# Attention and feed-forward kernel: fp16 split made in token order and turned by DMAs, denominators summed partly on TensorE

## The chip, the cores and the metric

The kernel runs on one core of one Trainium2 chip. The metric is the device time of one execution in microseconds (us). Engines are named as in the profile: PE is TensorE (PEld its weight loads), DVE is VectorE, ACT is ScalarE, POOL is GpSimd and SP is SyncE, whose queue (SPq) issues nearly all DMAs.

## What is computed

x is 8 x 512 x 1024 and the context is 8 x 512 x 256, in fp32. Cut to what matters, the reference is

```
q  = layernorm(x)                                # rows of 1024: 8 key heads x 4 query groups x 32
s  = q_head @ ctx_head.T / sqrt(32)              # 512 x 512 for each batch, key head and group
x1 = x + softmax(s) @ ctx_head
z  = layernorm(x1)                               # then 8 experts: one gate each, best one taken
out = x1 + (1 - g) * z + g * (bias[e] + degen[e] @ (update[e].T @ (z - debias[e])))
```

## The kernel before

**Units.** The attention is cut into 64 units (8 batches x 8 key heads). A unit has 16 score tiles of 128 keys x 512 queries, n = 0 to 15: four key blocks t for each of the 4 query groups. The unit loop is walked in four steps t = 0 to 3. For each score tile, TensorE makes it from 97 rows (`score_keys`, L589: fp16 high and low parts of both operands stacked, and one row with the shift that keeps the exponent small), ScalarE exponentiates it into `probs` (L884), and TensorE multiplies the probabilities with the values (`gather`, L603). The shift is the negative row maximum of approximate scores: TensorE makes them from the high parts alone (L551, four banks of PSUM), VectorE reduces them (`row_max`, L949), TensorE turns the 16 maxima (L634), ScalarE scales them (L795), and SP sends them by a small DMA into the last row of `q_stack` (`send_shift`, L406). This runs ahead: step t = 2 of unit u begins the maxima of unit u+2, and the shift of unit u+1 is sent within unit u.

**Denominators.** GpSimd adds the probability tiles of key blocks 0 and 1 (L363) and those of 2 and 3 (L351), 2048 columns each; TensorE sums both results over the keys with a matrix of ones (L616, L626), VectorE turns the total into `den_t` (L961) and inverts it (L967), and GpSimd scales the output rows and adds x (L323, L328).

**PSUM.** Four banks hold the approximate scores, one the output, and three banks serve by turns the score tiles, the turned maxima, the denominators and, before the change, the turned parts of x. A plan in the code (`filled`, `KEPT`, `bank_of`) gives each use its bank; TensorE waits (`bank_free`) until the use before it in that bank has been read.

**The split.** For each of the 32 token tiles of 128 rows: VectorE takes the moments, ScalarE centres x (L802) and scales it (L809), TensorE turns x and the context in ten 128 x 128 blocks (L577), ScalarE writes the high fp16 part times 16 (L820, L824) and VectorE the low part (L1002, L1008). Pairs of tiles are stored to DRAM (`q_split`, `k_split`) and loaded again by unit (`load_unit`, L68 to L76: 8 DMAs). Five tiles are made before the loop; the other 27 one per two units, the last in unit 51.

**SP's queue** runs a hand-written order: waits, then issues, one behind the other. The last stage (the feed-forward part) follows unit 63.

## Time and profile before

| what | value |
|---|---|
| median of 3 runs | 1024.77 us (1020.37 to 1025.66) |
| the profiled execution, first to last instruction (its span) | 1023.9 us |
| PE busy | 949.4 us (93%) |
| DVE busy | 904.8 us (88%) |
| ACT busy | 761.3 us (74%) |
| POOL busy | 794.4 us (78%) |
| SP queue | 161.76 MB, 64.3% of 16 DMA engines |

The profile gives no other time of the profiled execution than its span; the span lies 0.9 us under the median. Busy time of PE counts matmuls that overlap, so 93% is not 93% of its peak.

### The profile page before, as it was taken

The page shows a single profiled execution, that of the slowest core. Times are in us where ns is not written, and L with a number is a line of the kernel's source. Part 1 is how long each engine was busy: PE and PEld are TensorE (multiplying, and loading weights), DVE is VectorE, ACT ScalarE, POOL GpSimd, SP SyncE. Part 2 cuts the span into 40 slices and gives each one's busy share as a digit, 9 for nine tenths or more (in the row PEclk, how much of TensorE's full clock was granted, in tenths as well). Part 3 has the DMA queues.
Part 4 walks back from the last instruction along what each step waited for, and adds up shares of the span by engine and source line. Part 5 has one row for each costly group of instructions (what it writes and reads, how often), then busy time and mean ns, then how long its engine had stood idle before and what let it go on. Part 6 is the DMA issues. An engine that isn't in the chain of part 4 may idle for free.

```text
span 1023.9 us, 24706 instructions
## 1 busy us (share of the span) xinstructions
PE 949.4 (93%) x9518; PEld 372.5 (36%) x9518; DVE 904.8 (88%) x1138; ACT 761.3 (74%) x1333; POOL 794.4 (78%) x422
## 2 busy tenths in 40 slices
PE   4789999999999999999999999999999999999996
PEld 3223233333333232333333333332222226777773
DVE  6869999999999999999999999998888876888976
ACT  7468888888888888888888888888777777554440
POOL 7158999999999999999999999998999998222110
PEclk9989999999999999999999999999999999999998
DMA  7675677767677767676767686766555744766423
GB/s 247 184 167 114 161 154 168 156 162 159 155 158 167 168 152 170 145 171 150 180 143 175 138 188 134 182 122 154 119 119 139 165 95 141 247 213 236 148 104 164
DMA packets 319876, 164.19 MB, mean 160 GB/s; under 512 B 182216, under 2 KB 307240, under 8 KB 319760
## 3 DMA queue, kind: packets, MB, share of 16 engines
q1 hardware_dynamic: 319456, 161.76, 64.3%
q8 instruction: 76, 1.25, 0.5%
q0 software_dynamic: 304, 0.85, 0.3%
q14 instruction: 40, 0.33, 0.1%
HBM read 107.58 MB, written 54.53 MB: 158 GB/s over the span
## 4 chain that ended last, share of the span: by engine, by line
PE 36%; DVE 30%; issue 25%; ACT 5%; POOL 2%; DMA 1%; SPq 0%; DVEq 0%; POOLq 0%; ACTq 0%
DVE row_max L949 14%; PE psum L589 8%; PE psum L603 6%; PE psum L616 5%; PE psum L734 5%; DVE den_t L961 4%; PE psum L551 4%; ACT probs L884 3%; PE psum L712 3%; DVE o_t L955 3%; PE psum L577 2%; DVE probs L1161 2%; DVE prod_mem L1008 2%; PE psum L700 1%; ACT prod_mem L824 1%
## 5 line engine op out<-in xcount | busy, mean ns | idle before, releaser
L884 ACT ACTIVATE probs<-psum 128x512 f32<-128x512 f32 x1024 | 554.7, 596 | 106.7 <-PE psum L589 88.7
L949 DVE TENSOR_REDUCE row_max<-psum 128x4 f32<-128x2048 f32 x248 | 566.0, 2282 | 63.5 <-PE psum L551 63.1
L589 PE MATMUL psum<-q_stack,k_stack 97*32 97x512 f16 x4096 | 335.0, 386 | 10.2 <-issue 3.6
L363 POOL TENSOR_TENSOR sums<-probs 128x2048 f32<-128x2048 f32 x63 | 287.8, 4568 | 19.5 <-ACT probs L884 19.5
L351 POOL TENSOR_TENSOR sums<-probs 128x2048 f32<-128x2048 f32 x63 | 287.2, 4558 | 10.2 <-PE psum L626 5.5
L603 PE MATMUL psum<-probs,v_in 128*32 128x512 f32 x2048 | 268.9, 598 | 1.0
L589 PEld LDWEIGHTS psum<-q_stack,k_stack 97*32 97x32 f16 x4096 | 96.8, 95 | 258.7 <-ACT probs L884 148.6
L551 PE MATMUL psum<-high_mem 32*128 32x512 f16 x992 | 98.3, 385 | 23.7 <-DVE row_max L949 20.0
L323 POOL TENSOR_TENSOR o_t<-o_t,inv 128x512 f32<-128x512 f32 x64 | 67.1, 1048 | 44.2 <-DVE inv L967 44.2
L328 POOL TENSOR_TENSOR o_all<-o_all,o_t 128x512 f32<-128x512 f32 x64 | 81.5, 1274 | 9.5 <-POOL o_t L323 0.4
L603 PEld LDWEIGHTS psum<-probs,v_in 128*32 128x32 f32 x2048 | 59.4, 111 | 61.1 <-issue 16.7
L551 PEld LDWEIGHTS psum<-high_mem 32*128 32x128 f16 x992 | 26.8, 91 | 138.3 <-DVE row_max L949 83.2
L335 POOL TENSOR_SCALAR var_eps<-mv 128x1 f32<-128x1 f32 x32 | 9.3, 290 | 82.2 <-DVE mv L1036 81.6
L626 PE MATMUL psum<-sums,ones 128*32 128x512 f32 x512 | 68.1, 604 | 0.0
L734 PE MATMUL psum<-down,probs 128*128 128x512 f32 x128 | 64.3, 632 | 3.9 <-DVE probs L1161 3.1
L616 PE MATMUL psum<-sums,ones 128*32 128x512 f32 x512 | 67.5, 597 | 0.0
L712 PE MATMUL psum<-w_all,high_mem 128*128 128x136 f32 x512 | 64.8, 280 | 1.1 <-ACT high_mem L897 1.1
L712 PEld LDWEIGHTS psum<-w_all,high_mem 128*128 128x128 f32 x512 | 62.2, 191 | 5.2 <-issue 4.1
L577 PE MATMUL psum<-ident,xa 128*128 128x128 f32 x256 | 45.3, 310 | 16.0 <-ACT xa L809 10.5
L824 ACT ACTIVATE prod_mem<-psum 128x512 f16<-128x512 f32 x60 | 35.8, 597 | 32.0 <-PE psum L577 32.0
L897 ACT ACTIVATE high_mem<-psum 128x1024 f32<-128x1024 f32 x32 | 32.4, 1013 | 29.5 <-PE psum L700 29.5
L955 DVE STREAM_TRANSPOSE o_t<-psum 128x512 f32<-128x512 f32 x64 | 44.3, 692 | 8.2 <-PE psum L603 4.3
(120 smaller groups left out, 788.9 us busy)
## 6 DMA issues: line engine op xcount, KB each, us to landing
q_stack<-q_split SPq DMA_DIRECT2D x192, 128.0 KB, 3.4
xa<-in_x_dram SPq DMA_DIRECT2D x32, 512.0 KB, 4.7
o_all<-in_x_dram SPq DMA_DIRECT2D x256, 64.0 KB, 2.5
x_attended<-o_all SPq DMA_DIRECT2D x64, 256.0 KB, 4.1
out_dram<-probs SPq DMA_DIRECT2D x32, 512.0 KB, 2.9
q_split<-prod_mem SPq DMA_DIRECT2D x15, 1024.0 KB, 5.4
xa<-x_attended SPq DMA_DIRECT2D x16, 512.0 KB, 4.5
probs<-x_attended SPq DMA_DIRECT2D x16, 512.0 KB, 5.3
```

The costliest lines, as they stand in the source:

```text
L328: pool.tensor_tensor(o_all[:, half, :, h, :], o_all[:, half, :, h, :], turned_rows, ALU.add).then_inc(o_made, 1)
L351: pool.tensor_tensor(sums[:, (2 * u - 1) % SUMS], probs[:, (u - 1) % 2, 2], probs[:, (u - 1) % 2, 3], ALU.add).then_inc(back_done, 1)
L363: pool.tensor_tensor(sums[:, 2 * u % SUMS], probs[:, u % 2, 0], probs[:, u % 2, 1], ALU.add).then_inc(front_done, 1)
L551: last = pe.matmul(s_ps[:, g, :], q_high[rows, u % SLOTS, t * P:(t + 1) * P], k_high[rows, u % SLOTS, :], start=True, stop=True)
L589: last = pe.matmul(st_ps[row:row + D, bank_of["score", u, n], :], k_stack[:, u % SLOTS, t * P + row:t * P + row + D], q_stack[:, u % SLOTS ...
L603: last = pe.matmul(o_ps[g * D:(g + 1) * D, :], v_in[:, u % 2, t, :], probs[:, u % 2, t, g, :], start=(t == 0), stop=(t == ST - 1))
L616: pe.matmul(st_ps[g * D:(g + 1) * D, bank_of["den", u, 0], :], ones[:, 0:D], sums[:, 2 * u % SUMS, g, :], start=True, stop=False)
L712: last = pe.matmul(z_ps[:, t % 2, 0:WC], yT[:, t % 2, c, :], w_all[:, c, :], start=(c == 0), stop=(c == EC - 1))
L734: last = pe.matmul(result_bank(n)[:, half * 512:(half + 1) * 512], mixT[:, t, :], down[:, half * 512:(half + 1) * 512], start=True, stop=True)
L884: act.activation(probs[:, s, keys, g, :], st_ps[:, bank_of["score", u, n], :], ACT.Exp, scale=EXP_SCALE).then_inc(exped, 1)
L949: dve.reduce_max(row_max[:, u % 2, t:G * ST:ST], s_ps[:], AX.X).then_inc(reduced, 1)
L955: dve.transpose(o_t[:, u % 2, :], o_ps[:]).then_inc(o_taken, 1)
```

## The change

The split is made in token order: ScalarE writes the high part of the context (L846), normalises x in place in one pass that also multiplies by 16 (L851) and copies it to fp16 (L859). The low parts are subtractions: on VectorE for the first five tiles, on GpSimd (L284, L287, L291) for the others. Four DMAs per tile, issued by SP (`turn_x`, L410, and `turn_c`, L421), turn the fp16 parts; TensorE's ten transposes and the reads of PSUM behind them are gone. GpSimd adds only key blocks 0 and 1; TensorE sums blocks 2 and 3 straight from `probs`, so a unit has three groups of denominator matmuls (`denominators`, L667) in steps 0 and 1 of the following unit. The positions of the fp16 work among ScalarE's tiles, the bank plan, SP's order and the number of x tiles loaded ahead (6) are new; the folding of constants moves from before unit 0 into units 1 to 3.

```diff
+            C_SPLIT_AT, CENTRE_AT, HIGH_AT, SHIFT_AT = 4, 6, 2, 8
...
-                    filled += scores[half:]
...
                         filled.append(("den", u - 1, 0))
-            KEPT = {"score": 2, "max": 2, "den": (5, 5), "part": 6}
+                    if live(u):
+                        filled += [("score", u, n) for n in range(G * t, G * (t + 1))]
+            KEPT = {"score": 2, "max": 2, "den": 9}
             bank_of, bank_before, free_at, last_in = {}, {}, [0] * BANKS, [None] * BANKS
             for i, use in enumerate(filled):
...
+                def low_parts(n):
+
+                    pool.wait_ge(c_high, n + 1)
+                    pool.tensor_scalar(c_tile(n), c_tile(n), UP, None, ALU.mult).then_inc(c_scaled, 1)
+                    turned(pool, split_before(n), "c")
+                    pool.wait_ge(c_scaled, 2 * (n - FIRST) + 1)
+                    pool.tensor_tensor(c_parts(n)[:, 1], c_tile(n), c_parts(n)[:, 0], ALU.subtract
+                                       ).then_inc(c_scaled, 1)
+                    turned(pool, split_before(n), "x")
+                    pool.wait_ge(x_high, n + 1)
+                    pool.tensor_tensor(x_parts(n)[:, 1], x_tile(n), x_parts(n)[:, 0], ALU.subtract
+                                       ).then_inc(low_done, 1)
 
...
+                for u in range(-AHEAD, UNITS + 1):
+                    if u % 2 == 0 and whole(tile_of(u)) and u > -AHEAD:
+                        inverse_root(tile_of(u))
+                    if u % 2 == 1 and whole(tile_of(u)):
+                        low_parts(tile_of(u))
...
-                    if live(u - 2):
-                        normalise(u - 2)
...
-                        pool.tensor_tensor(sums[:, 2 * u % SUMS], probs[:, u % 2, 0], probs[:, u % 2, 1],
+                        pool.tensor_tensor(sums[:, u % SUMS], probs[:, u % 2, 0], probs[:, u % 2, 1],
                                            ALU.add).then_inc(front_done, 1)
...
+                    if live(u - 1):
+                        normalise(u - 1)
...
+                def turn_x(n, part):
+
+                    if part == 0:
+                        sp.wait_ge(x_high, n + 1)
+                        if n % 2 == 0 and n >= ST:
+                            sp.wait_ge(split_out, stored(n // 2))
+                    else:
+                        low_made(sp, n)
+                    landed = turned_first["x"][n] if n < FIRST else turned_in["x"][n % 2]
+                    cols = slice(n % 2 * P, (n % 2 + 1) * P)
+                    sp.dma_start_transpose(q_parts_of(n)[:, part, :, cols], x_parts(n)[:, part]).then_inc(landed, 16)
+
+                def turn_c(n):
+
+                    if n < FIRST:
+                        sp.wait_ge(c_low, n + 1)
+                    else:
+                        sp.wait_ge(c_scaled, 2 * (n - FIRST + 1))
+                    landed = turned_first["c"][n] if n < FIRST else turned_in["c"][n % 2]
+                    cols = slice(n % 2 * P, (n % 2 + 1) * P)
+                    for part in range(2):
+                        sp.dma_start_transpose(k_parts_of(n)[:, part, :, cols], c_parts(n)[:, part]
+                                               ).then_inc(landed, 16)
+
                 def load_first_highs(pair):
 
                     last = 2 * pair + 1
...
                 sp.wait_ge(early_out, 32)
                 load_unit(sp, 1, "highs")
                 load_unit(sp, 0)
                 load_v(0)
-                load_x(FIRST + 2)
+                turn_c(ST)
+                turn_x(ST, 0)
+                turn_x(ST, 1)
                 send_shift(0)
...
                 load_unit(sp, 2)
                 load_unit(sp, 3)
-
-                for u in range(-AHEAD, UNITS + 2):
+                sp.wait_ge(zeroed, 3)
+                sp.dma_start(down[NE:NE + NX, :], bias_w).then_inc(b_in, 16)
+                sp.dma_start(c_part[0:1, WC:WC + NX], imp_center.rearrange("(o n) -> o n", o=1)).then_inc(b_in, 16)
+                sp.dma_start(c_part[0:1, WC + NX:], imp_slope.rearrange("(o n) -> o n", o=1)).then_inc(b_in, 16)
+                for n in range(UPFRONT + 1, UPFRONT + FIRST):
+                    load_x(n)
...
+                        for g in ((2, 3), (), (0,), (1,))[u % HALF]:
+                            load_addend((u + 2) // HALF, g)
+                    if u % 2 == 0 and n + UPFRONT - 1 < TILES and u > -AHEAD:
+                        load_x(n + UPFRONT - 1)
+                    if u % 2 == 1 and whole(n):
+                        turn_x(n, 0)
+                        turn_x(n, 1)
+                        turn_c(n)
+                    if live(u) and live(u + 1):
                         send_shift(u + 1)
...
+                def denominators(u, i):
+
+                    if i == 0:
+                        bank_free("den", u, 0)
+                    terms = (probs[:, u % 2, 2], sums[:, u % SUMS], probs[:, u % 2, 3])[i]
+                    if i == 1:
+                        pe.wait_ge(front_done, u + 1)
                     else:
-                        pe.wait_ge(front_done, u + 1)
-                    bank_free("den", u, 0)
-                    wait(pe, den_taken, u)
-                    for g in range(G):
-                        pe.matmul(st_ps[g * D:(g + 1) * D, bank_of["den", u, 0], :], ones[:, 0:D],
-                                  sums[:, 2 * u % SUMS, g, :], start=True, stop=False)
-
-                def last_denominators(u):
-
...
-                        if u == -1 and t == 2:
-                            turn_max(0)
+                        if t == 2 and live(u + 1):
+                            turn_max(u + 1)
...
+                        if t == 0 and live(u - 1) and live(u):
+                            denominators(u - 1, 0)
+                        if t == 1 and live(u - 1) and live(u):
+                            denominators(u - 1, 1)
+                        if t == ST - 1 and live(u):
+                            gather(u, 1)
...
+                            score_keys(u, G * t, G * t + 2)
+                        if t == 0 and live(u - 1):
+                            gather(u - 1, ST - 1)
+                        if t == 1 and live(u - 1) and live(u):
+                            denominators(u - 1, 2)
+                        if t == 2 and live(u):
+                            gather(u, 0)
+                        if t == ST - 1 and live(u):
+                            gather(u, 2)
+                        if live(u):
+                            score_keys(u, G * t + 2, G * (t + 1))
 
...
+                def split_context(n):
+
+                    x_landed(act, n)
+                    if n >= ST:
+                        turned(act, split_before(n), "c")
+                    act.activation(c_parts(n)[:, 0], c_tile(n), ACT.Copy, scale=UP).then_inc(c_high, 1)
+
+                def normalise_tile(n):
+
+                    act.wait_ge(rstd_done, 2 * n + 2)
+                    act.activation(x_tile(n), x_tile(n), ACT.Identity, scale=rstd[:, n % 2:n % 2 + 1],
+                                   bias=neg_mean[:, n % 2:n % 2 + 1]).then_inc(xn_done, 1)
+
+                def high_part(n):
+
+                    act.wait_ge(xn_done, n + 1)
+                    if n >= ST:
+                        turned(act, split_before(n), "x")
+                    act.activation(x_parts(n)[:, 0], x_tile(n), ACT.Copy).then_inc(x_high, 1)
+
+                for n in range(FIRST):
+                    split_context(n)
+                    normalise_tile(n)
+                    high_part(n)
 
...
+                        if even and n == C_SPLIT_AT:
+                            split_context(tile)
+                        if even and n == CENTRE_AT:
+                            normalise_tile(tile)
+                        if odd and n == HIGH_AT:
+                            high_part(tile)
...
+                        if n == SHIFT_AT and live(u + 1):
                             make_shift(u + 1)
...
-                        if t == 0 and live(u - 2) and u % 2 == 0:
-                            take_denominators(u - 2)
...
-                        if t == 1 and live(u - 2):
-                            invert(u - 2)
...
+                        if t == 1 and live(u - 1) and live(u):
                             take_denominators(u - 1)
+                            invert(u - 1)
```

On TensorE, in the steps t = 0 and 1 of an even unit before the change (the rows begin in step 3 of the unit before; L616 and L626 are the denominators of that unit):

```order
L551 MATMUL psum<-high_mem 128x512 x4
L589 MATMUL psum<-q_stack,k_stack 32x512 x8
L603 MATMUL psum<-probs,v_in 32x512 x4
L634 MATMUL psum<-ident,row_max 16x128
L589 MATMUL psum<-q_stack,k_stack 32x512 x8
L616 MATMUL psum<-sums,ones 32x512 x4
L551 MATMUL psum<-high_mem 128x512 x4
L626 MATMUL psum<-sums,ones 32x512 x4
L589 MATMUL psum<-q_stack,k_stack 32x512 x8
```

Two groups of four denominator matmuls stood there, and the score tiles behind the second (L589) waited for probabilities to be read, not for the denominators. After the change the second and third group stand in step 1 of the unit (L637 is now `score_keys`; rows shown with what they wait for):

```order
L667 MATMUL psum<-sums,ones 32x512 [waits front_done]
L667 MATMUL psum<-sums,ones 32x512 x3
L637 MATMUL psum<-q_stack,k_stack 32x512 [waits exped]
L637 MATMUL psum<-q_stack,k_stack 32x512 x3
L637 MATMUL psum<-q_stack,k_stack 32x512 [waits exped]
L637 MATMUL psum<-q_stack,k_stack 32x512 x3
L667 MATMUL psum<-probs,ones 32x512 [waits exped]
L667 MATMUL psum<-probs,ones 32x512 x3
L637 MATMUL psum<-q_stack,k_stack 32x512 [waits den_taken]
L637 MATMUL psum<-q_stack,k_stack 32x512 x3
```

The third group sums `probs` directly; the second score tile pair of step 1 (tiles 6 and 7) comes straight behind it, and the plan gives tile 6 the bank of the denominators, so it waits until VectorE has read them (`den_taken`).

On SP, the last issues before the shift of unit 1 is sent (`send_shift(1)`, the last row; the same three-way load of a unit, 8 DMAs, stands ahead for unit 2, and 6 more for unit 1) were before the change:

```order
L68 DMA high_mem<-q_split 128x512
L69 DMA high_mem<-k_split 128x1x512
L74 DMA q_stack<-q_split 32x4x512 x3
L76 DMA k_stack<-k_split 32x512 x3
L431 DMA o_all<-in_x_dram 32x16x32 x4
L398 DMA q_split<-prod_mem 128x16x256
L400 DMA k_split<-k_parts 128x4x256
L412 DMA v_in<-in_ctx_dram 128x4x32
L406 DMA q_stack<-shift 1x16x128
```

After the change the loads of units 1, 2 and 3 stand as before behind `send_shift(0)`; between them and the rows below come three small constants and the loads of x tiles 7 to 10 (8 DMAs); then

```order
L477 DMA o_all<-in_x_dram 32x16x32 x8
L410 DMA_TRANSPOSE prod_mem<-xa 128x8x128 x2
L421 DMA_TRANSPOSE k_parts<-c_split 128x2x128 x2
L444 DMA q_split<-prod_mem 128x16x256
L446 DMA k_split<-k_parts 128x4x256
L458 DMA v_in<-in_ctx_dram 128x4x32
L477 DMA o_all<-in_x_dram 32x16x32 x8
L397 DMA xa<-in_x_dram 128x1024
L398 DMA cin<-in_ctx_dram 128x256
L452 DMA q_stack<-shift 1x16x128
```

Between `send_shift(0)` and `send_shift(1)` stood 29 DMAs, and now 58: the new ones are three constants, ten of x and context loads, 12 addends (`o_all`) and four transposing ones. Ahead of `send_shift(0)` stood 40 and stand 55.

## Rows read from the trace of the kernel before

**Rows 1.** Windows: busy us of PE, PEld, DVE, ACT, POOL, clock, DMA share.

```profile
400.00:500.00 100.00, 96.32 (x1064) 30.49 (x1064) 93.42 (x88) 84.11 (x155) 92.57 (x36) 1.00 0.71 159
...
700.00:800.00 100.00, 92.81 (x1072) 27.96 (x1072) 86.99 (x62) 74.62 (x143) 93.38 (x33) 1.00 0.62 138
```

**Rows 2.** Timeline of GpSimd, second addition of units two apart (start us, us).

```profile
408.36 4.56 POOL L351 TENSOR_TENSOR sums<-probs 128x2048 f32<-128x2048 f32 x1
...
433.68 4.56 POOL L351 TENSOR_TENSOR sums<-probs 128x2048 f32<-128x2048 f32 x1
...
760.40 4.57 POOL L351 TENSOR_TENSOR sums<-probs 128x2048 f32<-128x2048 f32 x1 [0.40 <-PE psum L626]
...
784.52 4.57 POOL L351 TENSOR_TENSOR sums<-probs 128x2048 f32<-128x2048 f32 x1 [0.40 <-PE psum L626]
```

**Rows 3.** Timeline of TensorE in units without split work.

```profile
757.85 1.05 PE L616 MATMUL psum<-sums,ones 128*32 128x512 f32 x8
758.83 0.39 PE L551 MATMUL psum<-high_mem 32*128 32x512 f16 x4
759.15 1.07 PE L626 MATMUL psum<-sums,ones 128*32 128x512 f32 x8
760.03 0.62 PE L589 MATMUL psum<-q_stack,k_stack 97*32 97x512 f16 x8
760.47 1.04 PE L603 MATMUL psum<-probs,v_in 128*32 128x512 f32 x8
761.33 0.77 PE L589 MATMUL psum<-q_stack,k_stack 97*32 97x512 f16 x8
...
774.16 0.40 PE L551 MATMUL psum<-high_mem 32*128 32x512 f16 x4 [0.52 <-DVE row_max L949]
...
777.04 0.40 PE L551 MATMUL psum<-high_mem 32*128 32x512 f16 x4 [0.65 <-DVE row_max L949]
...
778.78 0.28 PE L634 MATMUL psum<-ident,row_max 128*16 128x128 f32 x1
```

**Rows 4.** Timeline of VectorE in the same units.

```profile
771.18 0.70 DVE L961 STREAM_TRANSPOSE den_t<-psum 128x512 f32<-128x512 f32 x1
...
774.64 2.25 DVE L949 TENSOR_REDUCE row_max<-psum 128x4 f32<-128x2048 f32 x1
```

**Rows 5.** Timeline of ScalarE in the same units.

```profile
775.01 2.30 ACT L884 ACTIVATE probs<-psum 128x512 f32<-128x512 f32 x4 [0.46 <-PE psum L589]
```

**Rows 6.** Waits over the whole run (us in total, times, longest).

```profile
PEld psum L589 <- DVE den_t L961: 7.8, 36, 0.2
```

**Rows 7.** Groups by line over the whole run (busy us, mean ns, idle before).

```profile
L363 POOL TENSOR_TENSOR sums<-probs 128x2048 f32<-128x2048 f32 x63 | 287.8, 4568 | 19.5 <-ACT probs L884 19.5
...
L577 PE MATMUL psum<-ident,xa 128*128 128x128 f32 x256 | 45.3, 310 | 16.0 <-ACT xa L809 10.5 <-DVE prod_mem L1008 5.0
...
L1008 DVE SCALAR_TENSOR_TENSOR prod_mem<-psum,prod_mem 128x512 f16<-128x512 f32 x60 | 40.7, 679 | 3.1 <-ACT prod_mem L824 3.1
L802 ACT ACTIVATE xa<-xa,neg_mean 128x1024 f32<-128x1024 f32 x32 | 36.8, 1150 | 0.8 <-DVE var_eps L994 0.8
```

**Rows 8.** Timeline of SP's queue between the shifts of units 0 and 1.

```profile
41.22 0.57 SPq L406 DMA_DIRECT2D q_stack<-shift  x1
41.83 1.53 SPq L74 DMA_DIRECT2D q_stack<-q_split  x3
...
61.13 0.89 SPq L406 DMA_DIRECT2D q_stack<-shift  x1
```

**Rows 9.** Timeline of TensorE: first score tiles of units 0 and 1.

```profile
46.38 1.04 PE L589 MATMUL psum<-q_stack,k_stack 97*32 97x512 f16 x8
...
63.56 1.05 PE L589 MATMUL psum<-q_stack,k_stack 97*32 97x512 f16 x8 [3.64 <-issue]
```

**Rows 10.** Timeline of SP's queue in the middle of the loop.

```profile
406.57 2.14 SPq L400 DMA_DIRECT2D k_split<-k_parts  x1
...
416.03 2.17 SPq L431 DMA_DIRECT2D o_all<-in_x_dram  x4
...
421.09 0.38 SPq L68 DMA_DIRECT2D high_mem<-q_split  x1
...
425.06 0.42 SPq L412 DMA_DIRECT2D v_in<-in_ctx_dram  x1
```

373 lines of the change are left out of this document (142 added, 231 removed).

## The prediction

> **What bounds the kernel now.** I read the windows first, for the stages. Mid-loop PE is busy 96 of 100 us, VectorE 93, GpSimd 93 and ScalarE 84; in the units without split work 93, 87, 93 and 75 [rows 1]. No engine is alone the bound, so shares don't tell what a change is worth. The period does: GpSimd's second addition of the same unit parity comes at 408.36 and 433.68, 25.32 us for two units with one tile to split, and at 760.40 and 784.52, 24.12 us for two without [rows 2]. All the work of splitting thus costs 1.20 us per pair, whatever its busy time.
>
> Next the timelines of one unit, to see what a step is made of. TensorE's own lengths, start to start [rows 3]: the approximate scores 0.32 (758.83 to 759.15), a group of denominators 0.88 (0.98 ahead of approximate scores), two score tiles 0.44, a group of values 0.86. VectorE's reduction takes 2.25 and ends at 776.89; the next approximate scores start at 777.04, 0.15 us later [rows 3, 4]. From 774.16 to 777.04 that loop takes 2.88 us: the floor of a step, since the four banks of the approximate scores serve TensorE and VectorE by turns. Before, both limits lie close: steps of 2.9 to 3.4 us, by TensorE's content or this loop. ScalarE's tiles follow each other at (2.30 - 0.60)/3 = 0.57 us [rows 5], 9.1 us a unit, with room.
>
> What reading the denominators costs now: TensorE's score tiles waited for it 7.8 us in all, 0.2 us at most [rows 6]. They are read well before a score tile needs their bank.
>
> Last SP. Between the shifts of units 0 and 1 it sends 30 DMAs in 19.91 us (41.22 to 61.13), 0.66 us each, almost without a pause; the shift is needed, and unit 1's first scores start at 63.56, 2.43 us after its issue began [rows 8, 9]. At the start SP's queue sets the time.
>
> **The change part by part, a steady unit.** Removed from TensorE: 10 transposes a tile; added: one group of denominators a unit, 0.88 us. By content its four steps are now, in the order of the new code: step 0, scores 0.32, denominators 0.88, two tiles, values, two tiles, 2.94 us; step 1, 0.32 + 0.88 + 0.44 + 0.88 + 0.44 = 2.96; step 2 is short, and the loop with VectorE holds it at 2.88; step 3, 0.32 + 0.86 + 0.44 + 0.86 + 0.44 = 2.92.
>
> Two waits come on top. First, while the denominators hold one of three banks, score tiles have two. In step 0 the tiles start at 1.20; ScalarE takes the second from 2.21 to 2.81, TensorE wants its bank at 2.72: 0.14 us, step 0 is 3.08. Second, and larger: tile 6 stands right behind the third group and takes over the denominators' bank. In step 1 that group starts at 1.64 and ends 1.07 later, at 2.71 (length in [rows 3]); VectorE's reduction, begun 0.48 after the scores (774.16, 774.64), ends at 2.73, so it isn't late; it reads from 2.77 for 0.70 us [rows 4], TensorE resumes 0.15 us later, at 3.62 instead of 2.52. The 1.10 us is full loss, as no engine has work stored: the next approximate scores stand behind this wait. With two tiles and the turned maxima (issue taken as 0.21 from their 0.28 [rows 3]) the next step starts at 4.27. Before, this wait was 0.2 us at most. The unit: 3.08 + 4.27 + 2.88 + 2.92 = 13.15 us.
>
> Split work. ScalarE: one pass of 1.15 us less [rows 7]; of what is left, the context part and the normalising pass of even units lie in front of tiles 4 and 6, in ScalarE's idle time during the wait just described: nothing. The fp16 copy of odd units lies ahead of tile 2: tiles 2 and 3 come about 1.1 us later, so tiles 4 and 5 find their banks late and the third group starts about 0.45 us late, which moves the whole wait: +0.45 a pair. VectorE loses 0.68 us x 2 and a context part, work that hid in the reductions' gaps: no gain beside the 2.88 floor. GpSimd loses 4.57 us a unit and gets a low part; by its 512-column rate (half the 2048-column addition's 4.57 would be 1024 columns, 2.3 us [rows 7]) plus two context steps some 3.5 us a pair: about 18 of 26 us, and its remaining addition ends some 3 us before TensorE asks. Nothing, unless GpSimd has other waits. TensorE's transposes, 45.3 us in all [rows 7], are in the step sums already.
>
> So a pair takes 26.30 us, 26.75 with a tile, against 24.12 and 25.32. Units 1 to 51 are 25 pairs with a tile: 25 x 1.43 = 36; units 52 to 62, 5.5 pairs x 2.18 = 12. Sum +48 us.
>
> **The turning DMAs.** The trace has none. Below, one costs SP what a small DMA does, 0.42 us; above, what a held-up one does, 2.14 us [rows 10]. I take 0.66, the mean of SP's busy stretch, as these have 64 to 256 KB. In an odd unit SP loads a unit (421.09 to 425.06, 3.97 us), values 0.42, four addends 2.17 [rows 10]: 6.6 us; the low parts are ready at about 6.4; four turning DMAs 2.6, the shift 2.43 to be used: 11.7. It is needed at 13.15 + 1.20 = 14.35. Hidden, with 2.7 us of cover; at 2.14 each it arrives at 17.6 and costs 3.3 us a pair.
>
> Advanced Engine Details and Errata (the Trainium skill, section X-Bar Transpose) says that transposing DMAs are about as fast as plain ones. By that rule the 0.66 stands and the sum doesn't move; no row here shows it.
>
> **The start.** Ahead of the first shift stand 15 DMAs more, 0 to 15 x 0.66 = 10 us (SP also waited here, so some fit in); the turned parts now pass through DMAs before anything is stored or scored, so I take +8: first shift at 49.2. From there 58 DMAs instead of 29 stand ahead of the second: 59 x 0.66 = 39.2, shift 1 at 88.4, unit 1 at 90.8 against 63.56: +27 us. TensorE, ScalarE and VectorE all stop there: the score tiles that wait for the shift stand ahead of everything else on TensorE. Bounds: 59 x 0.42 with no delay ahead gives +5; 1.0 us each (the transfers of 10 loads held up) +50. Folding constants inside units 1 to 3 adds three waits of TensorE for a copy, some 1 us each: +3. The last stage is the same: 0.
>
> DMA: Bandwidth & Descriptors (the Trainium skill, section Issuing engines are not separate DMA queues) says that issue time is usually small against the transfer. That would leave out this term: rival 2 below has its time. Against it, here SP issues nearly without pause and the reader waits.
>
> **Sum.** 27 + 3 + 48 = 78. The profiled span is 1023.9, the median 0.9 above it: 1024.8 + 78 = 1103 us.
>
> **Rivals.** (1) Turning DMAs dear to issue, 2.14 us each: the shift is late in 25 odd units, 25 x 3.3 = 82, and 4 x 1.5 at the start: 1191 us. For it: SP has little room. Against: SP reads no data. It decides from about 1.3 us each. Chance 0.18. (2) Only one of the two new waits is real. Without the start term: 1076. Without the bank wait a pair is 24.1, 24.55 with a tile: 25 x -0.77 = -19, and with the start 1024.8 + 30 - 19 = 1036. For it: banks may come free otherwise than I count. Chance 0.20. (3) Faster: VectorE's read is early enough (the point is 1.1 us earlier in step 1), and SP's extra issues lie in its waits: 1024.8 - 19 + 3 = 1009, down to 985 if steps lose their other waits too. Against it: the order of code puts the read right ahead of tile 6, whatever the speeds. Chance 0.12. (4) Gains and losses cancel within 0.5%, about what a measurement of this kernel can tell from no change: 0.04. My forecast: 0.46, its own range 1075 to 1130.
>
> The range that leaves out 2 in 10: from 1022 (rival 3 and part of 4 below it) to 1180 (half of rival 1 above). Faster 0.12, same 0.04, slower 0.84.
>
> **What would show it.** The first score tiles of unit 1 at 85 to 95 us, with SP issuing from 50 on; GpSimd's additions 26 to 27 us apart per pair mid-loop and about 26.3 late; TensorE's score line waiting for `den_t` 62 times, some 1 us each, 60 to 70 us in all; shift DMAs issued before 12 us of an odd unit; GpSimd busy near 50%. The prediction is wrong if that wait is missing, if the period is under 25.3, or if a turning DMA occupies SP over 1.3 us.

## The result and the profile after

The changed kernel takes 1214.48 us (median of 4 runs, 1210.49 to 1218.13) against 1023.07 for the kernel before (median of 4, 1020.37 to 1025.66): 1.187 times, 95% interval 1.183 to 1.192. It is slower, as forecast, but by 191 us and not by 78, and above the range. The profiled execution took 1216.57 us, its span is 1214.8 us.

Read the period first, as in [rows 2]. GpSimd's one addition a unit is the mark (timeline of GpSimd, kernel after: start us, busy us, and in brackets the idle time before it):

```profile
564.91 4.56 POOL L378 TENSOR_TENSOR sums<-probs 128x2048 f32<-128x2048 f32 x1 [9.30 <-ACT probs L911]
578.48 4.55 POOL L378 TENSOR_TENSOR sums<-probs 128x2048 f32<-128x2048 f32 x1 [2.46 <-ACT probs L911]
591.96 4.56 POOL L378 TENSOR_TENSOR sums<-probs 128x2048 f32<-128x2048 f32 x1 [5.61 <-ACT probs L911]
611.81 4.55 POOL L378 TENSOR_TENSOR sums<-probs 128x2048 f32<-128x2048 f32 x1 [4.56 <-ACT probs L911]
626.50 4.55 POOL L378 TENSOR_TENSOR sums<-probs 128x2048 f32<-128x2048 f32 x1 [6.83 <-ACT probs L911]
...
1016.65 4.55 POOL L378 TENSOR_TENSOR sums<-probs 128x2048 f32<-128x2048 f32 x1 [6.41 <-ACT probs L911]
1030.05 4.57 POOL L378 TENSOR_TENSOR sums<-probs 128x2048 f32<-128x2048 f32 x1 [6.42 <-ACT probs L911]
```

Two kinds of units stand here. Late in the loop a unit takes 13.40 us. In the middle units of 13.57 and 13.48 us are followed by one of 19.85 and one of 14.69: 61.6 us for four, where before had 2 x 25.32 = 50.6 [rows 2]. The steady unit of the prediction (13.15 us) exists; a second thing comes on top of it once in four units. The windows say the same of the means, against [rows 1] (busy us of PE, PEld, DVE, ACT, POOL, granted clock, DMA share, GB/s): every engine is less busy, TensorE 82 of 100 us, and the bound is none of them.

```profile
400.00:500.00 100.00, 82.04 (x870) 23.29 (x862) 72.73 (x58) 63.29 (x119) 54.74 (x35) 0.95 0.78 160
700.00:800.00 100.00, 83.15 (x899) 23.85 (x903) 76.42 (x59) 64.41 (x121) 62.04 (x38) 0.97 0.73 148
```

**The clean unit.** TensorE, kernel after, from a score tile of step 0 to the start of step 2, to be set beside [rows 3]:

```profile
571.17 0.62 PE L637 MATMUL psum<-q_stack,k_stack 97*32 97x512 f16 x8
...
573.17 0.39 PE L614 MATMUL psum<-high_mem 32*128 32x512 f16 x4
573.49 1.07 PE L667 MATMUL psum<-sums,ones 128*32 128x512 f32 x8
574.37 0.78 PE L637 MATMUL psum<-q_stack,k_stack 97*32 97x512 f16 x8
574.98 1.03 PE L667 MATMUL psum<-probs,ones 128*32 128x512 f32 x8
576.86 0.61 PE L637 MATMUL psum<-q_stack,k_stack 97*32 97x512 f16 x8 [0.85 <-DVE den_t L984]
577.41 0.28 PE L686 MATMUL psum<-ident,row_max 128*16 128x128 f32 x1
577.62 0.39 PE L614 MATMUL psum<-high_mem 32*128 32x512 f16 x4
```

Step 1 runs from 573.17 to 577.62, 4.45 us where 4.27 were forecast. The third group of denominators ends at 576.01, and score tile 6 stands behind it until VectorE has read `den_t`. The list of waits (us in all, times, longest) has it 63 times. It lists matmuls (PE) and their weight loads (PEld) apart; the two overlap and aren't to be added up. [Rows 6] had 7.8 us for the weight loads:

```profile
PEld psum L637 <- issue: 221.8, 376, 24.2
...
PEld psum L637 <- DVE den_t L984: 110.3, 63, 1.8
...
PE psum L637 <- issue: 82.6, 25, 23.1
...
PE psum L637 <- DVE den_t L984: 53.1, 63, 0.8
```

The two rows with "issue" hold the second thing: score matmuls that wait for something for which the trace names no releasing engine. The matmuls do so 25 times, 82.6 us in all, the longest 23.1 us at the start. It is the shift, a row of the score stack that SP must send (experiment 2 moves nothing else).

**The long unit.** SP's queue and TensorE, kernel after (SP: start, us of issuing, DMAs). The shift of a unit is L452:

```profile
576.80 3.03 SPq L410 DMA_TRANSPOSE prod_mem<-xa  x2
579.87 3.11 SPq L421 DMA_TRANSPOSE k_parts<-c_split  x2
583.03 0.58 SPq L452 DMA_DIRECT2D q_stack<-shift  x1
...
592.47 5.05 SPq L477 DMA_DIRECT2D o_all<-in_x_dram  x8
...
598.57 0.59 SPq L452 DMA_DIRECT2D q_stack<-shift  x1
...
602.21 1.05 PE L637 MATMUL psum<-q_stack,k_stack 97*32 97x512 f16 x8 [3.80 <-issue]
603.01 1.95 PE L653 MATMUL psum<-probs,v_in 128*32 128x512 f32 x8
...
605.75 0.61 PE L614 MATMUL psum<-high_mem 32*128 32x512 f16 x4
```

Between two shifts SP issues almost without a pause for 15.5 us, longer than a clean unit: the stores of the turned pair, the eight loads of a unit, the values, eight addend loads, a tile and its context. The score tile starts 3.64 us behind the shift's issue, after a wait of 3.80 us. Issue isn't all of it: this shift took 3.5 us to land, those at 583.03 and 617.56 took 1.7. The DMA engines were busy 0.88 to 0.96 of the time behind this one, and 0.05 and 0.25 behind the other two (windows from 583 to 585 and from 617 to 620). No experiment takes this longer landing apart from the late issue. And the wait costs more than itself: what follows it runs slower. Windows of the kernel after:

```profile
598.00:602.00 4.00, 0.41 (x4) 0.00 (x0) 1.76 (x1) 0.00 (x0) 2.46 (x3) 0.87 0.88 231
602.00:604.00 2.00, 1.79 (x16) 0.72 (x20) 0.00 (x0) 1.05 (x3) 0.00 (x0) 0.50 0.96 213
```

The granted clock is 0.50 from 602 on, the 1.2 GHz level, and was back at 1.00 in the window from 608; TensorE had done hardly anything since 598.4. A group of values then takes 1.95 us, and 1.04 in the same place of other units. From the first late tile to the next step it is 3.54 us (602.21 to 605.75) where the clean unit takes 2.00; with what step 1 loses some 2.3 us.

**The turning DMAs.** The rows that the kernel before could not show, 60 of the 64 DMAs of each line (ns of issue on SP: least, median, most; the other eight have medians of 1322 and 1244):

```profile
L410 SPq DMA_TRANSPOSE prod_mem<-xa x60: 1231/1331/4798, 11.6 to 878.9; - x60
L421 SPq DMA_TRANSPOSE k_parts<-c_split x60: 1222/1248/2302, 9.0 to 881.6; - x60
```

1.33 us for one of 256 KB and 1.25 us for one of 64 KB, about twice the assumed 0.66. They land 3.8 and 2.4 us (medians) from their issue.

**The start.** SP and TensorE, kernel after, against [rows 8, 9]:

```profile
52.37 0.36 PE L601 MATMUL psum<-high_mem 32*128 32x256 f16 x1 [52.37 <-DMA high_mem<-probs]
...
67.01 0.59 SPq L452 DMA_DIRECT2D q_stack<-shift  x1
...
84.83 8.05 SPq L477 DMA_DIRECT2D o_all<-in_x_dram  x8
103.03 5.08 SPq L477 DMA_DIRECT2D o_all<-in_x_dram  x8
...
109.16 0.59 SPq L452 DMA_DIRECT2D q_stack<-shift  x1
...
112.64 1.04 PE L637 MATMUL psum<-q_stack,k_stack 97*32 97x512 f16 x8 [23.11 <-issue]
```

The first shift goes out at 67.01 instead of 41.22, the second at 109.16, and unit 1's first score tile starts at 112.64 instead of 63.56: +49 us. The first shift is late since its maxima are: the first row is TensorE's first approximate scores, which began at 27.36 before and now wait until 52.37 for parts that passed through turning DMAs.

**The budget.** GpSimd's first additions of unit 0 and of unit 62 start at 53.7 and 840.0 before and at 76.2 and 1030.0 after. So the span's +190.9 us are +22.5 up to unit 0's mark, +26.8 between the marks of units 0 and 1 (18.3 before, 45.1 after), +140.7 in the 61 units after that (768.0 and 908.7), and +0.9 behind the last mark.

### The profile page after: what moved, and what is told of

Read it like the earlier page. It is cut to its first block, busy times and chain, and to the rows that moved or that the text cites. A ratio compares the mean times of both kernels' runs of the same rounds, so it can differ in the third digit from the quotient of the medians.

```text
span 1214.8 us, 24979 instructions
## 1 busy us (share of the span) xinstructions
PE 971.3 (80%) x9702; PEld 352.8 (29%) x9702; DVE 892.2 (73%) x1020; ACT 715.5 (59%) x1269; POOL 614.4 (51%) x472
## 4 chain that ended last, share of the span: by engine, by line
PE 64%; DVE 20%; issue 9%; SPq 4%; DMA 2%; ACT 1%; POOL 1%; DVEq 0%; POOLq 0%; ACTq 0%
PE psum L637 17%; PE psum L667 15%; PE psum L653 15%; DVE row_max L972 12%; PE psum L614 7%; PE psum L778 4%; DVE den_t L984 4%; PE psum L756 3%; DVE probs L1172 2%; PE psum L744 1%; PE psum L686 1%; SPq L410 1%; DMA cin<-in_ctx_dram 1%; SPq L421 1%; SPq L76 0%
## 5 line engine op out<-in xcount | busy, mean ns | idle before, releaser
L637 PE MATMUL psum<-q_stack,k_stack 97*32 97x512 f16 x4096 | 347.9, 395 | 141.9 <-issue 82.6
L378 POOL TENSOR_TENSOR sums<-probs 128x2048 f32<-128x2048 f32 x63 | 287.2, 4559 | 323.6 <-ACT probs L911 323.6
L653 PE MATMUL psum<-probs,v_in 128*32 128x512 f32 x2048 | 279.8, 619 | 2.3 <-ACT down L823 1.3
L637 PEld LDWEIGHTS psum<-q_stack,k_stack 97*32 97x32 f16 x4096 | 106.4, 97 | 518.6 <-issue 221.8
L667 PE MATMUL psum<-probs,ones 128*32 128x512 f32 x1008 | 132.8, 599 | 0.0
L291 POOL TENSOR_TENSOR xa<-xa 128x1024 f16<-128x1024 f32 x27 | 57.7, 2137 | 83.9 <-ACT xa L859 83.9
L653 PEld LDWEIGHTS psum<-probs,v_in 128*32 128x32 f32 x2048 | 61.9, 112 | 45.4 <-ACT probs L911 15.6
L667 PE MATMUL psum<-sums,ones 128*32 128x512 f32 x504 | 71.3, 640 | 0.0
L984 DVE STREAM_TRANSPOSE den_t<-psum 128x512 f32<-128x512 f32 x64 | 45.9, 717 | 9.9 <-PE psum L667 8.0
L601 PE MATMUL psum<-high_mem 32*128 32x256 f16 x2 | 0.8, 376 | 53.7 <-DMA high_mem<-probs 52.4
```

The lines of the kernel that those rows point to most:

```text
L378: pool.tensor_tensor(sums[:, u % SUMS], probs[:, u % 2, 0], probs[:, u % 2, 1], ALU.add).then_inc(front_done, 1)
L637: last = pe.matmul(st_ps[row:row + D, bank_of["score", u, n], :], k_stack[:, u % SLOTS, t * P + row:t * P + row + D], q_stack[:, u % SLOTS ...
L653: last = pe.matmul(o_ps[g * D:(g + 1) * D, :], v_in[:, u % 2, t, :], probs[:, u % 2, t, g, :], start=(t == 0), stop=(t == ST - 1))
L667: last = pe.matmul(st_ps[g * D:(g + 1) * D, bank_of["den", u, 0], :], ones[:, 0:D], terms[:, g, :], start=(i == 0), stop=(i == 2))
L984: dve.transpose(den_t[:], st_ps[:, bank_of["den", u, 0], :]).then_inc(den_taken, 1)
```

## The experiments

Fourteen kernels ran; each is the kernel after with one edit, or a sum of such edits. The kernel before took 1022.6 to 1024.7 us (medians) beside them. Times are medians of 2 to 5 runs, and gains are counted from the 1214.5 us of the kernel after where nothing else is said.

**1. Take away the wait for the bank.** The planner keeps the denominators' bank for 11 score parts, and the turned maxima move behind the score tiles of step 2, so that tile 6 gets another bank.

```
-            KEPT = {"score": 2, "max": 2, "den": 9}
+            KEPT = {"score": 2, "max": 2, "den": 11}
...
-                        if t == 2 and live(u + 1):
-                            turn_max(u + 1)
...
+                        if t == 2 and live(u + 1):
+                            turn_max(u + 1)
```

> The bank of the denominators is given on later (kept 11 uses, so the turned maxima take it over, not score tile 6), and the maxima are turned behind the approximate scores of step 2. If the wait of tile 6 is what lengthens the clean units (13.4 us in the late stage), tile 6 no longer waits for den_t (163 us in all in the changed kernel), a clean unit takes 12.2 to 12.4 us, and the late units 52 to 62 alone give back 11 to 13 us; in the middle SP's queue may hold the units up instead, so the whole is 15 to 65 us faster. Rival: the units are held by VectorE's loop or TensorE's content, and the wait only shows where they would stop anyway: late units stay at 13.4 us, total within 10 us.

Measured: 1203.4 us, ratio 1.176 (1.172 to 1.179). TensorE's wait for `den_t` is gone from the list, and a late unit is 1.09 us shorter (timeline of GpSimd):

```profile
978.33 4.57 POOL L378 TENSOR_TENSOR sums<-probs 128x2048 f32<-128x2048 f32 x1 [5.32 <-ACT probs L911]
990.64 4.57 POOL L378 TENSOR_TENSOR sums<-probs 128x2048 f32<-128x2048 f32 x1 [5.33 <-ACT probs L911]
```

12.31 us against 13.40. But the whole gained only 11 us, under the 15 to 65 expected: in the middle a unit of 12.13 us was followed by ones of 14.50 and 19.65, so the gain was waited away at the next shifts. The wait is real, and this kernel can't price it.

**2. The shift first.** SP sends the shift right behind the values' load, ahead of stores, addends, tile loads and turning DMAs.

```
                     if live(u) and live(u + 1):
                         load_v(u + 1)
+                        send_shift(u + 1)
...
-                    if live(u) and live(u + 1):
-                        send_shift(u + 1)
```

> SP sends each shift right behind the load of the values, ahead of the addends, the x loads and the turning DMAs. If the shift's place in SP's queue is what costs the middle units 6 to 7 us per four units, most of it goes, 40 to 90 us in all, and the start (unit 1 at 112.6 us) comes 5 to 8 us earlier, as the eight addends and one x load of unit 0 no longer stand ahead. Rival: SP is simply full (over 50 of 60 us issuing per four units), the order moves the delay onto the unit loads and the total changes by under 20 us or grows.

Measured: 1188.3 us, ratio 1.161 (1.149 to 1.173), 26 us gained, where 40 to 90 were expected. One long unit in four is left. What holds it now, SP and TensorE of this kernel:

```profile
563.30 0.41 SPq L444 DMA_DIRECT2D q_split<-prod_mem  x1
...
572.42 0.60 SPq L452 DMA_DIRECT2D q_stack<-shift  x1
...
575.86 0.62 PE L636 MATMUL psum<-q_stack,k_stack 97*32 97x512 f16 x8 [2.70 <-issue]
```

The store of the turned pair, L444, starts 1.2 us behind the last turning DMA, when these have landed, and it, its fellow and the unit's loads still stand ahead of the shift.

**3 and 7. Thin out the start.** In the third the constants, the tiles 7 to 11 and the first 16 addends go behind unit 1's shift; in the seventh the same with tile 7 left ahead.

```
-                for n in range(UPFRONT + 1, UPFRONT + FIRST):
-                    load_x(n)
...
+                    if u == 0:
...
+                        for m in range(UPFRONT + 1, UPFRONT + FIRST):
+                            load_x(m)
+                        for g in (0, 1, 2, 3):
+                            load_addend(0, g)
```

> The three constants, the x loads 7 to 11 and the 16 addends of unit 0 go behind the shift of unit 1. If SP's queue sets the start, unit 1's first score tile comes at 80 to 90 us instead of 112.6 and the total is 20 to 30 us less. Rival: the loads and addends are needed at once behind it and the delay is only moved to unit 2 or 3: total within 8 us of the changed kernel.

> As e3_start, but x tile 7 is still loaded ahead, since VectorE's moments of that tile stood in front of unit 0's maxima and kept them waiting until 97 us. If the queue ahead of the second shift is what costs the start, unit 1 begins at 92 to 96 us instead of 112.6 and the total falls by 12 to 20 us; unit 2 may wait again, since the moved DMAs stand ahead of its shift. Rival: the whole stall moves to unit 2 as before and the total stays within 5 us.

Measured: 1214.7 us, ratio 1.187 (1.183 to 1.190), and 1213.9, ratio 1.185 (1.182 to 1.189): nothing. The timeline of TensorE, the seventh, shows where the gain went:

```profile
94.43 1.05 PE L642 MATMUL psum<-q_stack,k_stack 97*32 97x512 f16 x8 [6.35 <-issue]
...
121.78 1.04 PE L642 MATMUL psum<-q_stack,k_stack 97*32 97x512 f16 x8 [11.36 <-issue]
```

Unit 1 starts 18 us earlier (94.43 for 112.64), and unit 2 waits for its own shift behind the work put off. Work moved behind one shift on a full queue stands ahead of the next.

**4. Plain copies in place of the turning DMAs**, same bytes, same places; the parts are then not transposed.

```
-                    sp.dma_start_transpose(q_parts_of(n)[:, part, :, cols], x_parts(n)[:, part]).then_inc(landed, 16)
+                    sp.dma_start(q_parts_of(n)[:, part, :, cols], x_parts(n)[:, part].rearrange("p (h s) -> p h s", s=P)).then_inc(landed, 16)
```

> The 128 turning DMAs are plain copies of the same bytes to the same places, so the parts are not transposed and the result is not the attention's; the work and its order are the same. If what hurts is SP's time to issue a turning DMA (1.25 to 1.33 us each), each takes 0.45 to 0.6 us now, SP has 100 us less to issue, and the total falls by 60 to 110 us. Rival: what hurts is the bytes moved inside SBUF or the waits around them: the issue time falls but the total by under 30 us.

Measured: 1166.7 us, ratio 1.140 (1.137 to 1.143), 48 us gained, under the 60 to 110 expected; issue times of this kernel:

```profile
L410 SPq DMA_DIRECT2D prod_mem<-xa x60: 594/684/2514, 11.5 to 833.3; - x60
```

0.68 us, what I had assumed for a turning one. By medians the 128 DMAs give back 64 x 0.65 + 64 x 0.45 = 70 us of issue, and two thirds of it show in the time. Twice the price is a large cause, not the whole one.

**5. One turning DMA for the high and the low part together**, 64 instead of 128.

```
-                    sp.dma_start_transpose(q_parts_of(n)[:, part, :, cols], x_parts(n)[:, part]).then_inc(landed, 16)
+                    sp.dma_start_transpose(q_parts_of(n)[:, :, :, cols].rearrange("p l h s -> p (l h) s"),
+                                           x_parts(n).rearrange("p l e -> p (l e)")).then_inc(landed, 16)
```

> One turning DMA per tile for both parts of x and one for both parts of the context, 64 instead of 128, the same bytes. If a turning DMA costs SP a fixed 1.25 to 1.33 us, as the equal times for 256 KB and 64 KB say, each still takes 1.3 to 1.5 us, SP has 80 us less to issue, and the total falls by 30 to 60 us, as with the plain copies (49 us). Rival: the issue time grows with the blocks turned (16 instead of 8 in one DMA), each x one takes 2.6 us and the total stays within 15 us.

Measured: 1180.4 us, ratio 1.153 (1.149 to 1.156), 34 us gained.

```profile
L408 SPq DMA_TRANSPOSE prod_mem<-xa x30: 1788/2032/5372, 12.3 to 844.1; - x30
```

2.03 us for 512 KB against 2 x 1.33: part of the price goes by the DMA, part by its size.

**6. The addends issued by GpSimd**, which is idle half the time: `load_addend` moves from SP's program into GpSimd's, ahead of the tile's inverse root and low parts.

```
+                    if live(u + 2):
+                        for g in ((2, 3), (), (0,), (1,))[u % HALF]:
+                            load_addend((u + 2) // HALF, g)
```

> The 256 addend loads are issued by GpSimd (half idle) instead of SP; the bytes and the engines that move them are the same. If SP's issue time is what is short, SP loses 2.2 to 2.9 us a unit and the total falls by 50 to 90 us, the start included (16 addends stood ahead of the second shift, 8 to 13 us). Rival 1: the DMA engines are the limit and nothing changes, within 15 us. Rival 2: GpSimd takes about 1 us for each, 4 us a unit, and delays its own sums: the clean units rise above 13.6 us.

Measured: 1222.1 us, ratio 1.193 (1.188 to 1.199): no gain, and 8 us lost if anything, as the interval touches that of the kernel after (1.183 to 1.192). Unit 1's mark comes 4.6 us earlier, and the 61 units behind it take 8 us longer. GpSimd's timeline:

```profile
587.56 5.19 POOL L373 DMA_DIRECT2D o_all<-in_x_dram  x8
```

0.65 us each. In the even unit the tile's inverse root and mean stand behind these eight. ScalarE's normalising pass waits 1.98 us for them and TensorE 1.89 us for ScalarE, and the unit takes 15.39 us. In odd units the low parts come later behind four addends: SP's turning DMAs wait for them 14 times, 25.0 us in all, where the kernel after had one such wait of 0.4. That an engine is idle half the time doesn't make it a free queue.

**8. The edits 1 and 2 together.**

> The bank change (15 us when alone) and the earlier shift (30 us when alone) together. If the bank change gained little because SP held the middle units up, more of it shows now: clean units at 12.3 us, total 55 to 85 us below the changed kernel. Rival: SP is full, its work per four units (about 53 us) is a floor, and shorter units only wait longer: 35 to 45 us below, the sum of both or less.

Measured: 1159.7 us, ratio 1.132 (1.117 to 1.148). 55 us gained, where the two had given 11 and 26 apart. Still one unit in four is long, 15.4 to 18.9 us.

**9. The stores of the turned pair behind the shift too**, on top of 8.

```
-                    if u % 2 == 0 and (n - 1) % 2 == 1 and FIRST <= n - 1 < TILES:
-                        store_split(n - 1)
...
                         send_shift(u + 1)
+                    if u % 2 == 0 and (n - 1) % 2 == 1 and FIRST <= n - 1 < TILES:
+                        store_split(n - 1)
```

> As e8_bank_shift (shift sent right behind the v load, den word kept 11 parts), but the stores of the pair of turned tiles are issued behind the shift. In e8 one unit of four lasted 18.6 us: the sync engine's queue held two pairs of turning DMAs (5.2 us), then stood 2.5 us until they had landed, issued the stores (2.2 us), the eight loads of unit u+3 (5.5 us) and the v load, and only then the shift (617.67), and TensorE's next score tile came 4.84 us late. My theory: that wait and the stores are what makes the one long unit; without them the shift goes out 4.6 us earlier, the long unit drops to about 14 us, four units take 53 to 54 us instead of 57.3, and the time falls by about 55 us to 1100 us (1090 to 1115). Rival: the sync engine's pure issue time per four units (about 53 us) is already the bound, so the delay only moves to another unit: time 1130 to 1155. Second rival: what is late is the landing of the unit loads, not their issue: no change, 1160.

Measured: 1145.3 us, ratio 1.119 (1.113 to 1.125), 14 us under 8, with intervals that overlap. My theory missed by 45 us, and the number is the first rival's: that SP's issue time itself is near the bound. In the trace SP issues for 13.2 us a unit (400 to 700 us). The next two test it.

**10. Merged turning DMAs on top of 9** (the edit of 5), and **11. plain copies on top of 9** (the edit of 4).

> As e9_store_late, and each tile's high and low part are turned by one DMA, 2 per tile instead of 4. In e5 the merged one took 2.03 us to issue for x against 2 x 1.33, and about 1.3 to 1.5 for the context against 2 x 1.25, so four units cost the sync engine 3 to 4 us less. If the sync engine's issue time is the bound: 25 to 45 us faster than e9, about 1065 (1050 to 1085). If it no longer bounds in e9, only the start gains: 10 to 15 us, 1085.

> As e9_store_late, with the turning DMAs replaced by plain copies of the same bytes, so that the parts are not transposed and the output is not the reference's. 0.6 to 0.7 us each to issue instead of 1.25 to 1.33. This is about the floor of this order of work with all turning at the plain price: loop units 12.3 to 12.7 us, 1030 to 1060 us. If it stays above e10, something else than the issue time (landing, the clock) holds the loop.

Measured: 1096.1 us, ratio 1.071 (1.067 to 1.075), and 1093.6, ratio 1.070 (1.067 to 1.073). 49 and 52 us gained over 9, more than the 25 to 45 expected; the times themselves missed, 1096 against 1050 to 1085 and 1094 against the floor of 1030 to 1060. Both relieve SP by about 2 us a tile and both end at the same time, so SP's issue ahead of the shifts holds this loop. But single units stay long in 11 too (14 to 15.6 us), so the price of turning isn't all of it.

**12. The first 16 addends and the constants issued by GpSimd in unit 0**, on top of 10.

```
+                    if u == 0:
+                        for g in range(4):
+                            first_addend(0, g)
+                        pool.wait_ge(zeroed, 3)
+                        pool.dma_start(down[NE:NE + NX, :], bias_w).then_inc(b_in, 16)
...
-                    if live(u + 2):
+                    if live(u + 2) and u > 0:
```

> As e10_late_merged, and the first 16 addend loads and the three loads of constants are issued by GpSimd in unit 0 instead of by the sync engine ahead of the shift of unit 1. The sync engine has 19 DMAs fewer (about 12 us) there, so unit 1's first score tile should come 10 to 12 us earlier and the whole kernel end as much earlier: 1053 (1040 to 1065) if the start's delay is not merely moved on to unit 2, as it was in e3 and e7; if it is moved on, the same time as e10 within 3 us.

Measured: 1086.8 us, ratio 1.063 (1.059 to 1.067), 9 us under 10, with intervals that just touch; the 1040 to 1065 expected, counted from a faster 10, were missed. Here the start's delay isn't only moved, since the DMAs left SP's queue: unit 2's mark comes at 110.6 us, 7.6 earlier.

**13. The addends dealt out 4, 0, 8, 4** over four units instead of 8, 0, 4, 4, on top of 12.

```
-                        for g in ((2, 3), (), (0,), (1,))[u % HALF]:
+                        for g in ((3,), (), (0, 1), (2,))[u % HALF]:
```

> As e12_start_pool, with the 16 addend loads of four units dealt out as 4, 0, 8, 4 over the units instead of 8, 0, 4, 4, so that the unit which also holds the stores of the turned tiles and the x load has 4. In e12 the unit behind that burst still began 1 to 2 us late (TensorE waited 1.77 us for its shift at 599.97), once in four units: 15 times 1 to 1.5 us. Theory (the sync engine's bursts, not its mean load, are what is left in the loop): 10 to 20 us faster than e12, 1072 (1063 to 1080). Rival (the mean load is the bound): the delay moves to another unit, 1085 within 4 us.

Measured: 1066.7 us, ratio 1.043 (1.040 to 1.047), 20 us gained over 12 at the same number of DMAs: bursts ahead of a shift, not the mean load, were most of what was left. The timeline of GpSimd, this kernel:

```profile
668.72 4.57 POOL L397 TENSOR_TENSOR sums<-probs 128x2048 f32<-128x2048 f32 x1 [1.28 <-ACT probs L921]
681.82 4.56 POOL L397 TENSOR_TENSOR sums<-probs 128x2048 f32<-128x2048 f32 x1 [5.21 <-ACT probs L921]
693.95 4.56 POOL L397 TENSOR_TENSOR sums<-probs 128x2048 f32<-128x2048 f32 x1 [1.28 <-ACT probs L921]
```

13.10 and 12.13 us, a pair with a tile in 25.23 us, against 25.32 before [rows 2]. Not every pair is so: in 13 places of the loop a score tile still waits for its shift, 0.2 to 2.1 us.

**14. As 13, with the bank's wait put back** (the edit of 1 undone).

> As e13_spread, with the order of the changed kernel put back around the denominators' bank (kept 9 parts, the maxima's row turned ahead of the score tiles in step 2), so that score tile 6 again waits about 1.1 us for VectorE's den_t. It prices my prediction's steady term by itself, in a loop that the sync engine no longer holds. By the prediction's working: 62 units of about 0.8 to 1.1 us, 50 to 65 us slower than e13. Rival (the wait is absorbed, as it was in e1 where taking it away gave only 11 to 15 us): under 20 us slower.

Measured: 1108.1 us, ratio 1.083 (1.080 to 1.086), 41 us over 13, short of the 50 to 65 expected. GpSimd's timeline:

```profile
98.05 4.56 POOL L397 TENSOR_TENSOR sums<-probs 128x2048 f32<-128x2048 f32 x1 [4.93 <-ACT probs L921]
...
665.69 4.57 POOL L397 TENSOR_TENSOR sums<-probs 128x2048 f32<-128x2048 f32 x1 [2.47 <-ACT probs L921]
679.09 4.55 POOL L397 TENSOR_TENSOR sums<-probs 128x2048 f32<-128x2048 f32 x1 [5.52 <-ACT probs L921]
692.65 4.57 POOL L397 TENSOR_TENSOR sums<-probs 128x2048 f32<-128x2048 f32 x1 [2.47 <-ACT probs L921]
...
920.90 4.56 POOL L397 TENSOR_TENSOR sums<-probs 128x2048 f32<-128x2048 f32 x1 [6.42 <-ACT probs L921]
```

The list of waits of this kernel:

```profile
PEld psum L647 <- DVE den_t L994: 110.3, 63, 1.8
```

A pair takes 26.96 us, where the prediction had 26.75. Behind unit 1 no score tile waits for a shift any more. This is the loop that I forecast, without what SP does to it: its 61 units from the mark of unit 1 (98.05) to that of unit 62 (920.90) take 822.9 us.

## Why the prediction was wrong

**The sum, term by term.** By the marks, with experiment 14 as the loop without late shifts (it differs from the kernel after in what SP issues and in what order, and in 19 DMAs that GpSimd issues in unit 0; its clean units are those of the kernel after, 13.40 and 13.56 us): the start cost 49 us where 30 were forecast; the 61 units 822.9 - 768.0 = 55 us where 48 were forecast; late shifts 908.7 - 822.9 = 86 us where nothing was; the end 1 us. The step that failed is the third term; the price of a turning DMA, twice the assumed one, and the order on SP's queue are behind it.

**Right: the steady unit, in part by luck.** The wait of score tile 6 for `den_t` is there 63 times; step 1 is 4.45 us for 4.27, a clean pair with a tile 26.96 (experiment 14) for 26.75, a late unit 13.40 for 13.15. But the +48 was made of two parts, which rival 2 shows apart: the wait for the bank, 2.2 us a pair or +67 in all, and -19 for shorter steps. By the clean pairs of 14 and 13 (26.96 and 25.23 with a tile, 26.80 and 24.64 late) the wait is worth 25 x 1.73 + 5.5 x 2.16 = 55 us, and without it the pairs cost what they did before, +1 us in all and not -19. The two errors partly cancel. The 41 us between the times of 14 and 13 are less than 55, since the shorter units of 13 wait for shifts again. Experiment 1, taken alone, would have said 11: a wait is priced by taking it away only where nothing behind it waits longer.

**Wrong: the turning DMAs at 0.66 us each.** They take 1.33 and 1.25 us of SP. I had bounded the price by 0.42 and 2.14 and named 1.3 us as the point from which rival 1 decides; it fell on that point. I took the mean of SP's busy stretch because the sizes were alike, but no row of another kind of DMA shows the price of this one. Bringing it down, in experiments 4, 5, 10 and 11, is worth 34 to 52 us.

**Wrong: late shifts, put at nothing.** "Hidden, with 2.7 us of cover" was worked out for the odd unit, which holds the turning DMAs, and for no other. At the measured price the same working gives 6.6 + 5.2 + 2.4 = 14.2 us against 14.35: no cover is left. The trace agrees: in the odd unit above the shift goes out at 583.03 and its score tile starts 1.80 us behind it, just without a wait. So SP comes into the even unit with no lead, and there the new order puts eight addend loads and a tile load ahead of the shift, behind the stores and the unit's loads that stood there before too: 15.5 us in a unit of 13.4. Before, the shift was sent right behind the values' load, ahead of addends and tile loads, and the diff shows it moved.

Of the 86 us, 59.5 are waits of score matmuls for the shift (24 of the 25 in the list: 82.6 less the 23.1 at the start). The rest follows them, in the unit above some 2.3 us at the 1.2 GHz level, a term that the prediction didn't have. By marks the four units above have 61.6 - 2 x 26.96 = 7.7 us too much. That SP's order and price make the shifts late, and not GpSimd or VectorE, is shown by experiments 2, 10 and 13: none touches what another engine computes, and they gain 26, 49 and 20 us.

**Mis-sized: the start.** The mechanism held, SP issuing from the first shift to the second and all engines behind it. The sum was +27 and measures +49, near the bound that I had put at +50 for 1.0 us a DMA (by its own terms, with +8 ahead, it comes to +47), but by another way. From the first shift to the second 59 issues took 42.2 us (67.01 to 109.16), 0.71 each and not 0.66, so that part was nearly right, 42.2 for 39.2. Ahead of the first shift the loss was 26 us (67.01 for 41.22) where I had put +8. I had counted 15 DMAs more there, at 0.66 us. Of the 55 that now stand there 20 are turning ones, and these alone occupy SP for 32.7 us in the trace, with 3.8 us of standing until they have landed; TensorE's first approximate scores come 25.0 us later behind them. In experiment 13, with merged DMAs, most of that part is still there (first shift issued at 61.63). It was the shorter half of the paragraph and the larger error.

**Nothing, as forecast:** the last stage (+0.9 us), and GpSimd, busy 51% of the span.

**The rivals.** The time, 1214, lies nearest to rival 1 (1191), and its price of 1.3 us is the one that came. But its mechanism, a late shift in 25 odd units, is the smaller part of what the trace shows: 11 of the 24 waits are in odd units, 16.0 us of the 59.5. The rule that transposing DMAs are about as fast as plain ones (the Trainium skill, Advanced Engine Details and Errata, section X-Bar Transpose) holds here for the landing, 3.8 and 2.4 us (medians) against 4.6 and 3.1 for the plain copies of experiment 4, and not for what SP pays, 1.33 against 0.68 us for the same 256 KB. The rule that issue time is usually small against the transfer (the Trainium skill, DMA: Bandwidth & Descriptors, section Issuing engines are not separate DMA queues) holds here for one DMA, 0.49 us of issue against 2.8 to landing (medians of the addend loads). It would still have left out the larger part of this result, since the issues of one queue add up: 13.8 us a unit on average from 400 to 700 us, and 15.5 between the two shifts above.

**Still open.** The best version, experiment 13, is 4.3% slower than before. By the marks of its trace (unit 0 at 72.1, unit 62 at 879.8) 18 us of it lie ahead of unit 0, 6 us between units 0 and 1 (24.2 for 18.3), and 16 us in the 61 units behind. In its clean mid-loop pairs it is level with before (25.23 for 25.32), and late in the loop, where additions start at 867.47 and 879.79, it takes 12.32 us a unit, somewhat behind it (12.06). None of the fourteen is faster than before, and what turning by TensorE with only the new sums would do wasn't tried.

## What to carry to other kernels

Where one queue feeds a step that all engines wait for, add up all that it issues between two such feeds, for every kind of unit in the pattern and not only for the unit that the change adds to, and compare it with the length of that unit; what isn't urgent goes behind the feed, spread evenly. A new kind of DMA needs a price of its own, so measure one before 128 of them are built in, and merge them where the price goes mostly by the DMA. Gains of two waits that hide each other don't show one by one (11 and 26 us apart, 55 together): take away the longer one first, then price the shorter. And a sum that comes out near the measured one is checked part by part: +48 for +55 was +67 and -19 for +55 and +1.

## What the runs showed of the hardware

- A turning DMA occupies SP for 1.25 us at 64 KB and 1.33 us at 256 KB, and 2.03 us at 512 KB: nearly flat up to 256 KB. A plain copy of the same 256 KB took 0.68 us.
- The same loads cost SP 0.49 us (median, least 0.33, most 2.30) and eight in a row 5.05 us in the loop and 8.05 us at the start. GpSimd took 0.65 us each.
- A small DMA (the shift, 4 KB) landed in 1.7 us where the DMA engines were busy 0.05 and 0.25 of the time behind it, and in 3.5 us at 0.88 to 0.96.
- After 3.8 us without matmuls the granted clock was at 0.50 for some 5 us, in the middle of a loop that otherwise runs at 1.00: a late DMA cost 3.80 us of waiting and some 2.3 us more of slow matmuls.
